# A fused recurrence and routed feed-forward kernel: routing by single pairs, rows scattered from the third step, ten shared blocks ahead of the routed tiles

## The reference

```python
# first half: a diagonal recurrence
n = layernorm(x)
Bu = einsum('sd,bld->lbs', B, n)            # 64 states
h = a * h + bu_t                            # over the 512 positions, a = diagonal(A)
x = x + einsum('ds,lbs->bld', C, hs) + D * n
# second half: a shared and a routed SwiGLU network, F = 256, 8 experts
n = layernorm(x)
shared = silu(n @ sg.T) * (n @ su.T) @ sd.T
logits = n @ gate_w.T
top_id, score = argmax(logits), sigmoid(max(logits))
routed = swiglu(n * score, weights of expert top_id)
x = x + shared + routed
```

## Time and profile before

| what | value |
|---|---|
| median of 3 runs | 284.97 us (284.5 to 287.18) |
| profiled execution | 285.48 us, span 283.5 us |
| mean granted TensorE clock | 0.952 of full speed |
| TensorE busy | 236.5 us (83%), 1891 matmuls |
| VectorE busy | 176.7 us (62%) |
| ScalarE busy | 170.9 us (60%) |
| GpSimd busy | 148.2 us (52%) |

### The profile page before, as it was taken

One profiled execution on the slowest core, in us unless ns is written; L12 is line 12 of the kernel. 1 busy time (PEld: TensorE's weight loads), 2 busy tenths in 40 slices (PEclk: granted clock), 3 DMA queues, 4 the chain that ended last, 5 costly groups with the idle time before them and its releaser, 6 DMA issues.

```text
span 283.5 us, 6103 instructions
## 1 busy us (share of the span) xinstructions
PE 236.5 (83%) x1891; PEld 181.6 (64%) x1891; DVE 176.7 (62%) x510; ACT 170.9 (60%) x415; POOL 148.2 (52%) x152
## 2 busy tenths in 40 slices
PE   0596969878787299995999899999999999989940
PEld 0274646446446148671767699999999999747640
DVE  3699997999886846699523266555656556433310
ACT  2744898896896656321244988776867666333510
POOL 1000000047777777787730056777777777777930
PEclk9999799999999579996899999999999999999995
DMA  6999500012323232349339413654646433114992
GB/s 215 389 320 316 213 0 2 1 38 98 114 98 117 104 109 105 107 131 323 128 101 289 139 34 122 165 168 134 191 142 162 136 107 95 58 46 62 164 135 30
DMA packets 25918, 38.35 MB, mean 135 GB/s; under 512 B 3712, under 2 KB 17920, under 8 KB 25328
## 3 DMA queue, kind: packets, MB, share of 16 engines
q1 hardware_dynamic: 15264, 22.03, 25.1%
q0 software_dynamic: 10624, 15.93, 21.1%
HBM read 22.03 MB, written 20.25 MB: 149 GB/s over the span
## 4 chain that ended last, share of the span: by engine, by line
PE 60%; DVE 17%; ACT 12%; issue 5%; DMA 3%; POOL 0%; SPq 0%
PE bank L450 12%; PE bank L404 9%; PE bank L438 6%; PE bank L440 5%; PE bank L439 5%; PE bank L390 5%; PE bank L391 5%; PE bank L392 5%; ACT n L548 4%; ACT rows L562 4%; PE bank L411 3%; DMA rows<-in_x 3%; DVE stats L700 2%; DVE stats L737 2%; DVE rows L733 2%
## 5 line engine op out<-in xcount | busy, mean ns | idle before, releaser
L1027 POOL DMA_INDIRECT table<-rows,place x64 | 65.3, 1021 | 58.9 <-DVE place L801 40.0
L1068 POOL DMA_INDIRECT out<-w_full x51 | 49.3, 966 | 36.6 <-DVE w_full L997 21.9
L610 ACT ACTIVATE n1T<-bank,g_scale 128x512 f32<-128x512 f32 x32 | 22.0, 687 | 33.8 <-PE bank L392 27.7
L438 PE MATMUL bank<-xT_hi,w_split 128*128 128x256 f16 (+1 forms) x156 | 40.9, 264 | 0.7 <-DVE xT_lo L982 0.6
L440 PE MATMUL bank<-xT_hi,w_split 128*128 128x256 f16 (+1 forms) x156 | 40.9, 264 | 0.0
L439 PE MATMUL bank<-xT_lo,w_split 128*128 128x256 f16 (+1 forms) x156 | 40.7, 263 | 0.0
L949 DVE SCALAR_TENSOR_TENSOR hid<-bank,h_scale,n1T 128x512 f32<-128x512 f32 x32 | 23.6, 748 | 25.2 <-ACT n1T L610 20.7
L450 PE MATMUL bank<-w_full,hid 128*128 x284 | 38.5, 277 | 0.2 <-issue 0.2
L450 PEld LDWEIGHTS bank<-w_full,hid 128*128 128x128 f32 x284 | 34.8, 192 | 1.4 <-issue 0.5
L404 PEld LDWEIGHTS bank<-w_full,hid 128*128 128x128 f32 x256 | 31.6, 196 | 2.1 <-issue 0.3
L404 PE MATMUL bank<-w_full,hid 128*128 128x128 f32 x256 | 31.7, 279 | 0.0
(11 more groups left out here) (141 smaller groups left out, 436.5 us busy)
## 6 DMA issues: line engine op xcount, KB each, us to landing
w_full<-table SPq DMA_DIRECT2D x24, 264.0 KB, 2.9
rows<-in_x SPq DMA_DIRECT2D x8, 512.0 KB, 7.9
w_full<-in_weights SPq DMA_DIRECT2D x3, 1152.0 KB, 13.1
out<-rows POOLq DMA_DIRECT2D x10, 256.0 KB, 6.4
table<-in_pads SPq DMA_DIRECT2D x1, 2112.0 KB, 9.9
table<-in_pads SPq DMA_DIRECT2D x8, 264.0 KB
x_ring<-table SPq DMA_DIRECT2D x8, 264.0 KB, 3.7
table<-rows,place POOLq DMA_INDIRECT x64, 2.4
```

The lines of the kernel that those rows point to most:

```text
L438: mm(o, w_of(kind, e, 0, c), xT_hi[k][:, 0:w], start=True, stop=False)
L1027: g.indirect_dma_start(table[:, :], bass.IndirectOffsetOnAxis(ap=place[:, i:i + 1], axis=0), rows[:, i, :], None).then_inc(done, 16)
L1068: g.indirect_dma_start(out[:, :], bass.IndirectOffsetOnAxis(ap=x_in[k][:, s, 2 * D:2 * D + 1].bitcast(I32), axis=0), x_in[k][:, s, 0:D], N ...
```

## The change

`GROUP` becomes 1: 8 groups of 8 tiles, and the scratch tensors for the routing shrink with it. In step s the engines now do, for s from 2 on: route(s-2) on VectorE behind scan(s), places(s-2) behind residual(s), and ranks(s-2) and logits(s-1) on TensorE behind skip(s+1). GpSimd scatters the rows of pair s-3 in step s from step 3 on. The splits of the shared weights move into step 7 on VectorE, and block 0's gate and up stand on TensorE right behind the last y, transposes and ranks; the first two silus stand on ScalarE ahead of the square root of step 7, whose norm2 comes in two halves behind the silus of blocks 1 and 2. The last two groups' routing, the transposes of pair 7 (behind block 3), the routed weights' splits and the tile map (behind the products of block 7, instead of block 4) come later among the blocks. `MIDDLE` becomes 4, so 10 shared blocks lie ahead of the tiles and 6 behind.

```diff
@@ -28,8 +28,8 @@
 ROUTE = 5
 START = 3
 LATE = 10
-MIDDLE = 5
-GROUP = 2
+MIDDLE = 4
+GROUP = 1
 
 
 def columns(widths):
@@ -349,6 +349,7 @@
                     pe.wait_ge(s_parked, 2)
                 pe.wait_ge(s_lo, (g + 1) * GROUP * 2)
                 after(pe, s_before, g)
+                after(pe, s_picked, g)
                 for t in range(GT):
                     i = g * GT + t
                     tok = slice(i * P, (i + 1) * P)
@@ -382,10 +383,13 @@
 
             def shared_gate_up(b):
                 tok = slice(block_of(b) * SEQ, (block_of(b) + 1) * SEQ)
+                pe.wait_ge(s_lo, block_of(b) + 1)
                 for c in range(FC):
                     f = slice(P * c, P * (c + 1))
                     for kind, banks, used, done in ((0, gate_bank, s_silu, s_g), (1, up_bank, s_hid, s_u)):
                         after(pe, used, b * FC + (c - FC + 1))
+                        if b == 0 and c == 1 and kind == 1:
+                            pe.wait_ge(s_x1, LAST * 2 + 1)
                         o = banks[c][:]
                         mm(o, w_split[:, 0, kind, 0, f], n2T_hi[:, tok], start=True, stop=False)
                         mm(o, w_split[:, 0, kind, 0, f], n2T_lo[:, tok], start=False, stop=False)
@@ -466,35 +470,40 @@
                     skip(s + 1)
                 if s == 0:
                     weight_top()
-                if s >= 2 and s % GROUP == 0:
-                    logits(s // GROUP - 1)
-                if s >= 3 and s % GROUP == 1:
-                    ranks(s // GROUP - 1)
+                if s >= 2:
+                    ranks(s - 2)
+                if 1 <= s < LAST:
+                    logits(s - 1)
 
             pe.wait_ge(s_wlo, 2)
-            pe.wait_ge(s_w[2], 16)
             pe.wait_ge(s_n1T, PAIRS * 2)
             pe.wait_ge(s_h, PAIRS)
-            pe.wait_ge(s_x1, PAIRS * 2)
             for b in range(FIRST):
                 shared_gate_up(b)
-                if b == 0:
+                if b == 1:
+                    logits(GROUPS - 2)
+                    pe.wait_ge(s_w[2], 16)
+                    pe.wait_ge(s_x1, PAIRS * 2)
+                if b == 2:
+                    ranks(GROUPS - 2)
+                if b == 4:
+                    logits(GROUPS - 1)
+                if b == 5:
+                    ranks(GROUPS - 1)
+                if b >= 1:
+                    shared_down(b - 1)
+                if b == 3:
+                    pe.wait_ge(s_base, 2)
                     transpose_n2(LAST, 0)
                     transpose_n2(LAST, 1)
-                if b == 1:
-                    logits(GROUPS - 1)
-                if b >= 1:
-                    shared_down(b - 1)
-                if b == 2:
-                    ranks(GROUPS - 1)
-                if b == 3:
+                if b == 6:
                     counts()
 
             pe.wait_ge(s_map, MAP)
             pe.wait_ge(s_wlo, 4)
             load_expert(0)
+            transpose_tile(0)
             shared_down(FIRST - 1)
-            transpose_tile(0)
             transpose_tile(1)
             pe.wait_ge(s_silu, FIRST * FC)
             pe.wait_ge(s_hid, FIRST * FC)
@@ -555,14 +564,13 @@
                 after(act, s_y, q)
                 run(n1T[b][:], bank[b][:], ACT.Copy).then_inc(s_n1T, 1)
 
-            def norm2(q):
+            def norm2(q, b):
                 act.wait_ge(s_nb2, q + 1)
-                for t in range(PT):
+                for t in range(BT * b, BT * (b + 1)):
                     i = q * PT + t
                     last = run(n2[:, i, :], x1[:, i, :], ACT.Identity, bias=nb2[q % 2][:, t:t + 1],
                                scale=r2[q % 2][:, t:t + 1])
-                    if t % BT == BT - 1:
-                        last.then_inc(s_n2, 1)
+                last.then_inc(s_n2, 1)
 
             def split_hi(q, b):
                 act.wait_ge(s_t2, q * 2 + b + 1)
@@ -580,6 +588,20 @@
             def routed_weights_hi(k):
                 run(w_split[:, 0, k, 1:EW, :], w_full[:, k, F:].rearrange("p (e f) -> p e f", e=E), ACT.Copy,
                     scale=w_mul[:, 1 + k:2 + k]).then_inc(s_whi, 1)
+
...
 
             act.wait_ge(s_eps, 3)
             run(warm[:], eps1[:], ACT.Sqrt)
@@ -596,27 +618,18 @@
                     copy_n1T(s + 1, 1)
                 if s >= 1:
                     split_hi(s - 1, 1)
+                if s == LAST:
+                    shared_silu(0, 0)
+                    shared_silu(1, 1)
                 if s >= 0:
                     std2(s)
-                    norm2(s)
                 if s == 1:
                     router_hi()
+                if 0 <= s < LAST:
+                    norm2(s, 0)
+                    norm2(s, 1)
                 if 1 <= s < 3:
                     shared_weights_hi(s - 1)
-
...
 
             def tile_score(j):
                 tiles = range(j, min(j + 2, TILES))
@@ -649,20 +662,23 @@
                 w = FC * width(j)
                 run(silu[j % 2][:, 0:w], gate_bank[j % 2][:, 0:w], ACT.Silu, scale=g_scale[:, 0:1]).then_inc(r_silu, 1)
 
-            for b in range(FIRST):
+            for b in range(1, FIRST):
                 shared_silu(b * FC, 0)
                 shared_silu(b * FC + 1, 1)
-                if b == 0:
+                if b in (1, 2):
+                    norm2(LAST, b - 1)
+                if b == 3:
                     split_hi(LAST, 0)
                     split_hi(LAST, 1)
-                if b in (1, 2):
-                    routed_weights_hi(b - 1)
-                if b > EARLY:
+                if b in (4, 5):
+                    routed_weights_hi(b - 4)
+                if EARLY < b < FIRST - 1:
                     late_base(b - 1)
 
             tile_score(0)
             tile_scale(0)
             tile_scale(1)
+            late_base(FIRST - 2)
             tile_hi(0)
             tile_score(2)
             tile_scale(2)
@@ -850,14 +866,30 @@
                                        scalar=w_mul[:, 1 + k:2 + k], in1=w_split[:, 0, k, 1:EW, :],
                                        op0=ALU.mult, op1=ALU.subtract).then_inc(s_wlo, 1)
 
...
+
             v.memset(half[:], 0.5).then_inc(s_eps, 1)
             v.memset(eps1[:], LN_EPS).then_inc(s_eps, 1)
             v.memset(eps2[:], LN_EPS * X_SCALE ** -2).then_inc(s_eps, 1)
             for s in range(-2, PAIRS):
                 if s >= 0:
                     scan(s)
-                if s >= 4 and s % GROUP == 0:
-                    places(s // GROUP - 2)
+                if s == 2:
+                    router_lo()
+                if s >= 2:
+                    route(s - 2)
                 if s == 1:
                     powers_of_two()
                 if s + 2 < PAIRS:
@@ -866,10 +898,19 @@
                     router_max()
                 if s == 0:
                     weight_max(1)
+                if s == LAST:
+                    shared_weights_lo(0)
+                    shared_weights_lo(1)
                 if s >= 0:
                     residual(s)
+                if s == LAST:
+                    dve.wait_ge(s_scale, 3)
+                    shared_hidden(0, 0, 0)
+                    shared_hidden(1, 1, 0)
                 if s == 1:
                     scales()
+                if s >= 2:
+                    places(s - 2)
                 if s >= 1:
                     split_lo(s - 1)
                 if s >= 0:
@@ -878,13 +919,6 @@
                     norm1_scales(s + 2)
                 if s == -1:
                     weight_max(0)
-                if s == 2:
-                    router_lo()
-                if s >= 3 and s % GROUP == 1:
-                    route(s // GROUP - 1)
-            for k in range(2):
-                shared_weights_lo(k)
-
             def tile_map():
                 steps = [0]
 
@@ -942,38 +976,26 @@
                 ready(v.tensor_scalar(tile_weights[:], tile_expert_f[:], float(F), None, ALU.mult))
                 assert steps[0] == MAP
 
...
-
-            dve.wait_ge(s_scale, 3)
-            places(GROUPS - 2)
-            for b in range(FIRST + 1):
+            for b in range(1, FIRST + 1):
                 if b < FIRST:
                     shared_hidden(b * FC, 0, b)
                     shared_hidden(b * FC + 1, 1, b)
-                if b == 0:
-                    split_lo(LAST)
+                if b == 1:
+                    route(GROUPS - 2)
+                if b == 2:
+                    places(GROUPS - 2)
                 if 1 <= b <= EARLY:
                     base(b - 1)
-                if b == 1:
+                if b == 3:
+                    split_lo(LAST)
+                if b == 4:
                     route(GROUPS - 1)
-                if b == 2:
+                if b == 5:
                     places(GROUPS - 1)
-                if b == 4:
+                if b in (6, 8):
+                    routed_weights_lo((b - 6) // 2)
+                if b == 7:
                     tile_map()
-                if b in (3, 5):
```

(65 more changed lines are left out.)

## The result

The changed kernel takes 298.62 us (median of 4 runs, 297.75 to 301.08), against 284.74 before on the same chips: ratio 1.0535, 95% interval 1.0426 to 1.0644. It is slower, by 13.9 us where 10 were forecast; 298.62 lies in the range. Its profiled execution has a span of 295.6 us, 12.1 more than before.

The account below looks back on a forecast made before the run. TensorE bounds the routed tiles; a ring of ScalarE, TensorE and VectorE bounds the steps. First tile 5.6 us later plus 4.4 of tail gave 10.0 on the profiled 285.48: 295.5, median 295.0; range 287.5 to 301.

Parts of the forecast that it names:

- The ring: In the steps, places waits for ranks behind skip: 13.48 us from norm2 to norm2, 67.4 for five steps against 50.71.
- The rival of a covered ring: Skip is done before VectorE reaches places, so the wait for ranks vanishes: 279 us, chance 0.12.
- Ranks and places: Two terms of each step's sum: 0.55 us for two ranks matmuls with hand-over, 0.47 for places at half width.
- The term of norm2 and norm1: Term of each step's sum: norm2, norm1 and a square root on ScalarE, 6.36 us.
- the rival of the slow clock: TensorE waits in each step and skip runs at half clock, 1.2 us per step: 301 us, chance 0.10.
- VectorE's work per step: About 10.9 us of VectorE work in a step, hidden under 13.48, the bound if the wait for ranks is covered.
- The blocks: Shared blocks from 107.1 us; block 7 starts at 140.3, map at 144.7; half clock at the start up to 2.8.
- The table loads: ScalarE loads its table three times instead of once around step 7, 1.28 us each: no cost by the row.
- From the map to the loads: Map at 144.7, pads in 11.2 us later at 155.9, where tile loads start.
- The rival of quicker pads: Pads land sooner, so tile loads wait for the last scatter or block instead: 290 us, chance 0.14.
- The seam: Transpose of tile 2: 5.7 us after the first tanh plus 1.4 for half clock, 166.7 against 161.09 before.
- The tail: One shared block moves from ahead of the routed tiles to behind them, where TensorE is the bound: 4.37 us.

Follow-up runs that it names:

- e2: The changed kernel with places(s-2) moved to stand last in step s on VectorE, behind both scales: 287.51 us, ratio 1.0126 to the kernel before.
- f1: The changed kernel with ranks ahead of skip on TensorE, places last in the step on VectorE, and MIDDLE 5 (eleven shared blocks ahead): 279.65 us, ratio 0.9837.
- e1: The changed kernel with the two ranks matmuls ahead of skip on TensorE in steps 2 to 6: 290.81 us, ratio 1.0245 to the kernel before.
- e3: The changed kernel with MIDDLE 5, eleven shared blocks ahead of the tiles instead of ten: 294.60 us.
- g1: The kernel of f1 unchanged, taken again on another chip with five rounds: 280.17 us, ratio 0.9837 to the kernel before.
- g2: The kernel of f1 with the tile map in two parts, the second routed-weights split one block later, and MIDDLE 6: 277.95 us, ratio 0.9768.

## Why the prediction was right, and where it was off

- *The ring.* 13.48 us a step were forecast; measured are 13.9, 13.7, 13.3, 14.3 and 13.1, in all 68.4 against 67.4. Moving either end of the new wait gave 8 to 11 us back, so the cause is shown and not only the size. The rival of a covered ring is out. That the sum comes out within 1 us is in part luck. Ranks and places took 0.86 from the first ranks matmul to split_lo (45.41 to 46.27) instead of 1.02, 0.8 less in five steps. The term of norm2 and norm1 was 0.6 and 0.4 longer in the first two steps, most of it the split of the shared weights (line 586) that ScalarE does there and the sum left out. And the clock cost 1.0 in one step.
- *The clock in the steps.* In slices of 10 us from 30 to 100, TensorE's granted clock was 0.76 to 0.89 in six and 1.00 in one; before it was 0.94 in the first and 1.00 in the next five. With the ring opened at its other end (e2) it fell in two of seven. In the step of 14.3 one bu took 2.63 us instead of 1.94:

```profile
68.69 1.94 PE L318 MATMUL bank<-n1T,const 128*64 128x512 f32 x4
...
82.29 2.63 PE L318 MATMUL bank<-n1T,const 128*64 128x512 f32 x4
```

There the way from the first n1T copy to the first skip matmul took 3.56 instead of 2.59, and in the other four steps 2.58 to 2.61: that is the 1.0. Skip, which the rival has at half clock, took 2.05 in every step; the half clock fell on y (1.5 to 2.1 instead of 1.16) and on transposes, for which the ring does not wait in the other steps. So the rival of the slow clock is true in kind, and cost 1 us, not 6. The measured 298.62 lies nearer to its 301 than to the 295.0 of the forecast, but did not come about in its way.
- *VectorE's work per step*, 10.9 in the forecast as the bound behind the ring, is 10.72 where the ring is open (f1).
- *The blocks.* Block 7 (140.85) and the map came within 0.6 us of the working. Half clock at their start cost 0.6 of the possible 2.8; the wait for pair 6 (0.7 in the sum) did not come, and the one for pair 7 was 0.98. The table loads cost nothing here, as forecast: TensorE waits nowhere from 107.33 to 125.8.
- *From the map to the loads*: this is the term that was mis-sized. 11.2 us from the map's first instruction until the pads are in were read off the fall of the DMA traffic, and the loads were put right behind; measured are 12.7 (145.22 to 157.96). It is 0.86 to the first issue, 7.83 for the eight issues (to 153.91), 3.40 until the last pad is in (157.31), and 0.65 until SyncE issues the first load, for which the sum had nothing. The trace of before could have told: there the pads' semaphore takes its last step at 137.32, 13.5 us after the map's start and 2.3 after the fall at 135. With 0.5 from the map's start this is all of the 2.1 us by which loads were late. The rival of quicker pads is out.
- *The seam.* 7.3 us from the first tanh to the transpose of tile 2, against 7.1. The half clock was there: the last down took 3.52 instead of 1.95, 1.6 where 1.4 were put.
- *The tail.* 4.3, against 4.37.
- *From the trace to the median.* The measured 298.62 is 3.6 above the forecast 295.0. The late seam is 2.2 of it. The other 1.4 is in no stage: the forecast set the median 0.5 under the profiled execution, as in the kernel before, and here it lies 0.9 above it (297.75).

## What to carry to other kernels

When an engine's list gets a new wait in the middle, follow the ring: what stands behind the waiting instruction, who waits for that, and whether the producer itself stands behind something that these feed. Here five steps grew by 17.7 us, to 68.4. With both ends of the wait moved, and the same work, they take 53.3: the place of two small instructions in VectorE's list and two matmuls in TensorE's cost 15.1 us, 3 in each step, and the work of the smaller groups the other 2.6. A stage that many conditions gate (scatters, pads, map, splits, TensorE) has to be read with all of them: starting the pads 3.1 us earlier gave 1.3, and twice the edit pushed another condition (the second split, the map) into last place. And blocks that can be moved belong into the hole that a chain leaves ahead of a stage, measured after the chain is settled: here an eleventh block in the hole also kept the work behind it at full clock (1.95 us for the last down instead of 3.5 to 3.6).

## What was not expected of the hardware

The eight pad stores (264 KB each, from HBM to HBM) landed in 4.0 us in the median. From the end of their issues to the first tile load it took 3.8 to 4.75 us in seven kernels whose loads waited for them last (the changed one 4.05, e1 3.78, e2 4.75, e3 3.94, f1 3.95, g1 3.79, g2 3.84); some 0.65 us of that is SyncE's own way to the first load. It is a price behind the map that the kernel before, bound by its scatters, did not show in its time.

ScalarE's table loads show no time beside their own. The timeline of the changed kernel around the end of the steps:

```profile
110.09 0.69 ACT L595 ACTIVATE n1T<-bank,g_scale 128x512 f32<-128x512 f32 x1 [0.15 <-PE bank L396]
110.79 1.28 ACT L550 ACT_TABLE_LOAD   x1
112.09 0.30 ACT L550 ACTIVATE sd<-var,eps 128x8 f32<-128x8 f32 x1
112.41 1.28 ACT L595 ACT_TABLE_LOAD   x1
113.70 1.27 ACT L595 ACTIVATE n1T<-bank,g_scale 128x512 f32<-128x512 f32 x2
```

Each load starts within 0.03 us of the end of the instruction ahead, takes 1.28, and the next starts 0.02 behind. The drain of 1.38 us that the Trainium skill (ScalarE: Activation LUTs, What ACT_TABLE_LOAD costs) adds is not to be seen; the measured rows decide.
